# Attention and mixture-of-experts kernel: inputs stored with a column of ones for the second matmul, all turned operands copied by VectorE

## The reference

```python
xh = x.reshape(B, T, H, hd)                          # H = 16 heads, hd = 8
x_centered = xh - jnp.mean(xh, axis=1, keepdims=True)
corr = softmax(einsum('bthd,bThd->bhtT', x_centered, x_centered))
out = einsum('bhtT,bThd->bthd', corr, xh)            # second matmul, uses x uncentred
x = _layernorm(x + out)
...                                                  # routing: 8 of 64 experts per token
x = _layernorm(x + experts(x) + shared_expert(x))
```

## Time and profile before

| | |
|---|---|
| median of 3 runs | 610.99 us |
| the profiled execution's own time | 613.51 us |
| its span, first to last instruction | 611.4 us |
| TensorE matmul busy | 414.1 us (68%), 2948 instructions |
| VectorE busy | 344.1 us (56%), 1127 instructions |
| ScalarE busy | 382.1 us (62%), 515 instructions |
| GpSimd busy | 374.4 us (61%), 401 instructions |

### The profile page before, as it was taken

The page is one execution under the profiler, slowest core; times in us unless marked ns, Lnnn a source line. Parts: engine busy times, 40 slices in busy tenths (PEclk is TensorE's granted clock), DMA queues, the critical chain, the costliest instruction groups (busy, mean ns, idle before and its releaser), DMA issues.

```text
span 611.4 us, 8799 instructions
## 1 busy us (share of the span) xinstructions
PE 414.1 (68%) x2948; PEld 196.6 (32%) x2948; DVE 344.1 (56%) x1127; ACT 382.1 (62%) x515; POOL 374.4 (61%) x401
## 2 busy tenths in 40 slices
PE   4798899899898998998997974255065656632000
PEld 4323233233333333333332312243064545521000
DVE  5422767777687686796783565864034333332075
ACT  2599899998998998998999972013043222210046
POOL 3000003777776776767767777777707888888755
PEclk9699999999999999999999995567568677566555
DMA  3699991101000000000000000000066555333597
GB/s 103 182 242 292 222 234 43 58 23 26 12 12 19 7 21 8 3 21 6 3 20 6 2 20 2 20 1 2 1 191 122 89 88 63 35 34 35 69 303 213
DMA packets 83122, 43.64 MB, mean 71 GB/s; under 512 B 13319, under 2 KB 82707, under 8 KB 83072
## 3 DMA queue, kind: packets, MB, share of 16 engines
q1 hardware_dynamic: 61568, 36.18, 23.3%
q0 software_dynamic: 21504, 6.81, 9.7%
HBM read 21.27 MB, written 44.40 MB: 107 GB/s over the span
## 4 chain that ended last, share of the span: by engine, by line
PE 27%; POOL 25%; ACT 21%; issue 13%; DVE 9%; DMA 4%; SPq 0%; ACTq 0%; DVEq 0%; POOLq 0%
ACT large L898 15%; POOL sums L511 15%; POOL records L493 10%; PE PV L663 8%; PE S L649 6%; PE M L567 3%; ACT OT L883 2%; PE PV L673 2%; PE M L555 2%; PE M L596 1%; DMA sums<-centred,target 1%; ACT LR L876 1%; PE S L567 1%; PE M L590 1%; DVE last_stats L1487 1%
## 5 line engine op out<-in xcount | busy, mean ns | idle before, releaser
L493 POOL DMA_INDIRECT records<-rec,index x256 | 253.3, 990 | 183.1 <-DVE index L1297 106.5
L898 ACT ACTIVATE large<-S,shift_now 128x1024 f32<-128x1024 f32 x256 | 275.0, 1123 | 25.0 <-PE S L649 24.2
L663 PE MATMUL PV<-large,V 128*9 128x512 f32 x1024 | 134.8, 599 | 0.2 <-ACT large L898 0.2
L511 POOL DMA_INDIRECT sums<-centred,target x64 | 99.5, 1554 | 36.4 <-issue 18.9
L649 PE MATMUL S<-LR 64*128 64x512 bf16 x512 | 99.8, 392 | 20.4 <-ACT large L898 17.4
L649 PEld LDWEIGHTS S<-LR 64*128 64x128 bf16 x512 | 24.2, 93 | 158.4 <-ACT large L898 121.5
L1154 DVE COPY LR<-M 128x1024 bf16<-128x1024 bf16 x42 | 28.7, 684 | 23.5 <-PE M L567 23.5
L1454 DVE CAST target<-number 128x4 uint32<-128x4 f32 x16 | 2.7, 171 | 62.9 <-DMA sums<-centred,target 62.0
L795 PE MATMUL PV<-ident,AK 128*128 128x128 f32 x32 | 9.2, 383 | 42.7 <-DVE AK L1429 42.6
L963 ACT COPY AK<-S 128x512 f32<-128x512 f32 x16 | 9.3, 583 | 44.8 <-PE S L777 44.8
L1002 ACT ACTIVATE last_log<-last_moments,eps 128x4 f32<-128x4 f32 x8 | 2.4, 297 | 45.9 <-DVE last_moments L1490 45.9
(11 more groups left out here) (181 smaller groups left out, 703.8 us busy)
## 6 DMA issues: line engine op xcount, KB each, us to landing
records<-blank SPq DMA_DIRECT2D x1, 6176.0 KB, 29.7
X<-records SPq DMA_DIRECT2D x16, 386.0 KB, 3.6
large<-sums SPq DMA_DIRECT2D x24, 256.0 KB, 4.4
sums<-blank SPq DMA_DIRECT2D x2, 2112.0 KB
large<-L_ffn_w_dram SPq DMA_DIRECT2D x2, 2048.0 KB, 18.9
records<-rec,index POOLq DMA_INDIRECT x256, 2.1
X<-L_attn_x_dram SPq DMA_DIRECT2D x8, 256.0 KB, 2.7
sums<-Z SPq DMA_DIRECT2D x8, 256.0 KB
```

The source lines that it names most:

```text
L493: pool.indirect_dma_start(records, bass.IndirectOffsetOnAxis(ap=index[:, i * TOP + k:i * TOP + k + 1], axis=0), rec[:, i, :], None, bounds ...
L511: pool.indirect_dma_start(sums[n % SUMS], bass.IndirectOffsetOnAxis(ap=target[:, u, i:i + 1], axis=0), ye[:, u, i, :], None, bounds_check= ...
L663: mm = pe.matmul(PV[g % 2][32 * i:32 * i + VCOLS, :], V[:, 2 * c + k, QUAD * g + i, :], E[:, u % 2, i, k, :], start=c == 0 and k == 0, sto ...
L898: nc.scalar.activation(E[:, u % 2, 2 * (i // 2):2 * (i // 2) + 2, i % 2, :], S[:, 2 * (n % 2):2 * (n % 2) + 2, :], ACT.Exp, bias=shift_now ...
```

## The change

X gets nine columns per head instead of eight and is laid out as tile, column, head: a head's eight channels are 16 words (64 bytes) apart. The ninth column, of ones, is filled once by GpSimd. The host passes the input with channels ordered by column and head, so the load still moves 512 contiguous bytes per row. V, its two copies per batch and its waits are gone: `weigh` takes its stationary operand from X, nine words 64 bytes apart. VectorE's two instructions that read X, the subtraction of the mean (L1093) and the addition to O (L1157), read it through the view `by_head`, whose neighbouring words are 64 bytes apart. lr3 and lr6 are copied by VectorE.

```diff
-ACT_TAKES = {3: 11, 6: 15}
...
-        X = sb("X", [P, BATCHES * TILES * DIM])
-        V = sb("V", [P, TILES, HEADS, VCOLS])
+        X = sb("X", [P, BATCHES * TILES * VCOLS * HEADS])
...
+        def inputs_of(q):
+
+            return X[:, q * TILES * VCOLS * HEADS:(q + 1) * TILES * VCOLS * HEADS].rearrange(
+                "p (i c h) -> p i c h", i=TILES, c=VCOLS)
+
+        def by_head(q):
+
+            return inputs_of(q)[:, :, 0:HD, :].rearrange("p i c h -> p i h c")
...
-            fill(V[:, :, :, HD:VCOLS], 1.0)
+            fill(X[:, :].rearrange("p (i c h) -> p i c h", c=VCOLS, h=HEADS)[:, :, HD, :], 1.0)
...
-                    mm = pe.matmul(PV[g % 2][32 * i:32 * i + VCOLS, :], V[:, 2 * c + k, QUAD * g + i, :],
+                    mm = pe.matmul(PV[g % 2][32 * i:32 * i + VCOLS, :], inputs_of(b)[:, 2 * c + k, :, QUAD * g + i],
...
-                v.tensor_tensor(xc[:, :].rearrange("p (i d) -> p i d", i=TILES),
-                                tokens_of(X, q).rearrange("p (i d) -> p i d", i=TILES),
-                                M[bank][:, 0:DIM].unsqueeze(1).to_broadcast([P, TILES, DIM]),
-                                ALU.subtract).then_inc(read[bank], 1)
+                v.tensor_tensor(xc[:, :].rearrange("p (i h c) -> p i h c", i=TILES, c=HD), by_head(q),
+                                M[bank][:, 0:DIM].rearrange("p (c h) -> p h c", c=HD).unsqueeze(1)
+                                .to_broadcast([P, TILES, HEADS, HD]), ALU.subtract).then_inc(read[bank], 1)
...
-                                            tokens_of(X, p), ALU.add))
+                                            O[:, :, :].rearrange("p i (h c) -> p i h c", c=HD), by_head(p), ALU.add))
...
                     post_shared_out(phase, b, p)
+                if with_prep:
+                    take_turned(phase, b, 3)
+                if with_post:
                     post_record(p, t)
...
                 if with_prep:
+                    take_turned(phase, b, 6)
                     take_turned(phase, b, 7)
```

More of the change, by code:

```diff
@@ L257, in post_norm_block @@
         pv_read = sem("pv_read")
-        v_built = sem("v_built")
         shift_taken = sem("shift_taken")
@@ L384, in _ @@
                     sp.wait_ge(x_loaded, 16 * q)
-                sp.dma_start(tokens_of(X, q).rearrange("p (i d) -> p i d", i=TILES),
+                sp.dma_start(inputs_of(q)[:, :, 0:HD, :].rearrange("p i c h -> p i (c h)"),
                              x[q].rearrange("(i p) d -> p i d", p=P)).then_inc(x_loaded, 16)
@@ L554, in mean @@
                 for i in range(TILES):
-                    mm = pe.matmul(M[m][:, 0:DIM], mean_w[:, :], tokens_of(X, q, i, 1), start=i == 0, stop=i == TILES - 1)
+                    mm = pe.matmul(M[m][:, 0:DIM], mean_w[:, :],
+                                   inputs_of(q)[:, i, 0:HD, :].rearrange("p c h -> p (c h)"), start=i == 0, stop=i == TILES - 1)
                 mm.then_inc(written[m], 1)
@@ L657, in weigh @@
                 if k == 0:
-                    if u in (0, UNITS - 2):
-                        wait_next(pe, v_built, 2 * b + (1 if u == 0 else 2))
                     if c == 0 and (g >= 2 or not isinstance(b, int) or b > 0):
@@ L865, in exp_logits @@
                                      ).then_inc(read[bank], 1)
[L867 to L876, removed]
             def copy_quad(b, g):
@@ L906, in batch @@
                                 copy_quad(b - 1, QUADS - 1)
[L907 to L918, removed]
                     if phase != "first":
@@ L1156, in post_norm @@
             def post_norm(p, t):
-                t.step("y", v.tensor_tensor(O[:, :, :].rearrange("p i d -> p (i d)"), O[:, :, :].rearrange("p i d -> p (i d)"),
-                                            tokens_of(X, p), ALU.add))
+                t.step("y", v.tensor_tensor(O[:, :, :].rearrange("p i (h c) -> p i h c", c=HD),
+                                            O[:, :, :].rearrange("p i (h c) -> p i h c", c=HD), by_head(p), ALU.add))
                 t.after("y")
@@ L1507 @@
     for name in _INS:
-        a = np.ascontiguousarray(inputs[name])
+        a = inputs[name]
+        if name == "L0_attn_x":
+            a = np.reshape(a, (BATCHES, TOKENS, HEADS, HD)).transpose(0, 1, 3, 2).reshape(BATCHES, TOKENS, DIM)
+        a = np.ascontiguousarray(a)
         arrays[f"{name}_dram"] = a
```

## The result

The changed kernel takes 614.26 us (median of 20 runs, 611.76 to 617.01) beside 611.39 us for the kernel before (20 runs). The ratio is 1.0047 with a 95% interval of 1.0035 to 1.0060: it is slower by 2.9 us, as forecast (+3.6). The profiled execution has a span of 613.9 us (before: 611.4). In the profiles after, exponential n, A and the slots are named as before.

A forecast was written before the change was run, and what follows sets the result against it. ScalarE and TensorE were taken to bound it in turn, then VectorE's own order. 0.15 us without strides plus 3.5 us for strides gave +3.6 on 610.99, 614.6 us; likeliest 613 to 616.5, 8 in 10 within 609 to 617.

The forecast's parts named there:

- Exponential 1 to A: Up to ScalarE's release of VectorE, after which VectorE runs its own order: first V copy's removal saves 0.40 us, second's nothing.
- Strides: VectorE's two readings of X 64 bytes apart: each 0.53 us longer, 0.49 on the path per batch, 3.5 us in all.
- `most` at A+11.51, the scores of exponential 26 at A+12.26: After VectorE's release by ScalarE: `most` starts 0.76 us late behind lr3's copy; exponential 26 begins 0.1 us later.
- A to the next `mean`: From ScalarE's release of VectorE onward: +0.69 us, 0.53 from lr3's place and 0.16 from lr7 behind lr6.
- A middle batch: Whole middle batch of the attention: 0.29 us longer before strides, +0.78 us with them.
- The weight loads: TensorE's loads of nine strided words: taken as 0, staying near 88 ns; high end 0.3 us a batch.
- Batch 0: First attention batch, with no work of a batch before it and VectorE free: -1.18 us.
- The end: GpSimd's scatters of batches 5 to 7: 0.32 us of slack before batch 6's closes; +0.15 us overall without stride costs.
- Free strides: Rival for VectorE's strided readings: no cost, 611.1 us, no measurable change; chance 0.34 with partial stride costs included.
- ScalarE's time reaching the end: Rival at slot 12: lr3's copy precedes `most`, so ScalarE's saving survives, -7 us, 604 us; chance 0.15.
- The strided loads: Rival: TensorE's weight loads pay too, +1.9 us on the forecast, 616.5 us; chance 0.08 shared with the no-lift rival.
- That the change doesn't lift ScalarE at all: Rival: V's 0.40 us per batch is lost too, 617.0 us; chance 0.08 shared with the strided-loads rival.

The follow-up runs named there:

- before_few: Kernel before, with only the first 12 of a batch's 32 scatters issued; batch 43.47 us.
- storage_few: Changed kernel with VectorE's two readings of X contiguous in storage order and only 12 of 32 scatters per batch; batch 43.70 us.
- two_layouts: Kernel before, with the second matmul's weights taken from a second SBUF layout of the input, loaded by DMA, and V gone; 608.68 us, ratio 0.9953.
- y_few: Changed kernel with 12 of 32 scatters per batch and only the addition to O reading X contiguously; batch 43.70 us.
- lr7_first_few: Changed kernel with 12 of 32 scatters per batch and VectorE copying lr7 before lr6; batch 43.91 us.
- lr3_back: Changed kernel with the copy of lr3 back on ScalarE; 611.58 us, ratio 1.0001.
- layout_only: Changed kernel with the copies of lr3 and lr6 back on ScalarE, leaving only X's layout changed against the kernel before; 611.08 us, ratio 0.9998.
- packed_few: Changed kernel with 12 of 32 scatters per batch and nine neighbouring words of X as the second matmul's weights; batch 43.98 us.
- copies_only: Kernel before, with only the copies of lr3 and lr6 moved to VectorE; 614.41 us, ratio 1.0042.
- after_few: Changed kernel with only the first 12 of a batch's 32 scatters issued; batch 44.05 us.

## Why the prediction was right, point by point

- *Exponential 1 to A, -0.40 us.* Right: 20.21 to 19.83 without strides (0.38 us), in before_few against storage_few and again in two_layouts. Both V copies are gone and no more than the first one's 0.40 us came, so the second gave nothing, as forecast.
- *Strides, +0.53 us, 0.49 on the path.* The mechanism is right, the size too large: 0.35 to 0.37 us, and 0.35 on the path, where I had 0.49. The step that was mis-sized is the 2.1 ns taken from L1139 for each place. 512 words at 64 bytes cost 0.37/512 = 0.7 ns more than neighbours, nearer to the 0.5 ns of L1169 that I set aside as too few words. (A piece of L1139 is eight words of bf16, so its 2.1 ns were not the price of the jump alone.) That the subtraction is covered was right (y_few). Its 0.53 us in the prologue can't be read from these traces, since the first copy of the shift starts anywhere from 16.85 to 18.67 us in them.
- *`most` at A+11.51, the scores of exponential 26 at A+12.26.* Measured 184.15-172.58 = 11.57 and 184.84-172.58 = 12.26. The saving of lr3's copy became a wait of 0.76 us there, and exponential 26 began at A+12.69 instead of A+12.50, 0.19 us late where I had 0.1 (0.12 without meetings: 12.63 beside 12.51).
- *A to the next `mean`, +0.69 us.* Measured +0.60 without GpSimd's meetings and +0.56 as run. I split it 0.53 and 0.16. The 0.16 for lr7 behind lr6 is right (lr7_first_few, and lr3_back beside layout_only); lr3's place costs 0.42 to 0.45. Without meetings VectorE reads `most` 0.60 us later, as I had it (from A+12.84 to A+13.44), but lr5 comes only 0.44 us later (from A+16.68 to A+17.12) where I had 0.53. The batch that I had read also held a long `wsum` (0.43 us at 183.05), which I took for VectorE's own work; in the changed kernel it is short in batches 3 to 6, which gives a part of the delay back.
- *A middle batch, +0.78 us with strides.* Measured +0.56 (0.58 without meetings). What I had too much is 0.14 us for the stride and 0.1 us from the last point.
- *The weight loads, 0.* They took 101 ns instead of "near 88", and packed_few prices that at 0.07 us per batch, well below my high end of 0.3.
- *Batch 0, -1.18 us.* From its first copy of the shift to the `mean` of batch 1: 42.53 us after, 43.55 before, -1.02, in one execution each, both with a granted clock of 0.50 from 20 to 30 us.
- *The end.* GpSimd's first scatter of batch 5 comes at 321.42 us, 2.92 later than before. That the 0.32 us of slack ahead of batch 6's closes is seen in copies_only and lr3_back, where its first scatter starts 0.30 us behind the one before it. It closes in the changed kernel too, but there the last scatter of batch 5 had waited 1.21 us for a DMA. The last scatter of all ends at 445.59 us beside 442.27: +3.3, where I had +3.6. What comes behind it is 168.3 us long beside 169.2 before and 167.8 to 169.1 in the other kernels with all scatters, whatever their change.
- *What I did not have* is VectorE and GpSimd meeting: batch 2 of the changed kernel is 0.74 us longer by it, batch 4 of the kernel before 0.26. In this profiled execution it makes up for the strides that I priced too high, so a part of the closeness of +3.6 to +2.9 is luck. How many batches meet in the timed runs the profile of one can't say.
- *The rivals.* Free strides fall by 1056 ns instead of 691. ScalarE's time reaching the end falls at `most`, which waited 0.81 us for VectorE. The strided loads are real but small. That the change doesn't lift ScalarE at all falls by two_layouts, which gained the 0.38 us.

## What to carry to other kernels

When two engines are both nearly full, work taken off the busier one counts only up to the next wait that ends on another engine. Ask what the copy is next in line for: here ScalarE released a PSUM bank at the right moment, and VectorE, less busy on average, let `most` begin 0.8 us late, because the copy came behind 10 us of its own order. And look at the start of each period for a job that stands ahead of what the other engine waits for; moving one such job gave 0.7 us per batch, where removing both V copies gave 0.38. And before two traces are compared, see whether an instruction between the marks is longer in one of them: `wsum` alone had mixed up the prices of lr3 and lr6.

## What the runs showed of the hardware

TensorE's granted clock in batch 0 isn't the same in every execution. From 20 to 30 us it was 0.50 (1.2 GHz) in the profiles before and after and 1.00 (2.4 GHz) in after_few, whose instructions up to there are the changed kernel's. The rows of the changed kernel and then of after_few:

```profile
20.00:25.00 5.00, 3.58 (x14) 2.05 (x14) 1.37 (x2) 1.98 (x2) 0.00 (x0) 0.50 0.60 175
25.00:30.00 5.00, 4.29 (x20) 0.61 (x24) 3.51 (x9) 3.94 (x5) 0.00 (x0) 0.50 1.10 264
```

```profile
20.00:25.00 5.00, 2.86 (x22) 1.58 (x26) 2.79 (x5) 3.71 (x4) 0.00 (x0) 1.00 0.67 206
25.00:30.00 5.00, 4.69 (x40) 1.14 (x38) 3.22 (x8) 5.00 (x6) 0.00 (x0) 1.00 1.10 261
```

In both, TensorE has been idle for 2.6 us before the first scores (at 20.94 and 20.56 us). Batch 0 took 41.57 us at the one level and 38.96 at the other. These 2.6 us are as large as the effect studied here: single profiled spans of these kernels can't be compared, their middle batches can.

The meetings of VectorE and GpSimd were the other thing I had not expected: 0.13 to 0.28 us on each `tensor_scalar` or cast that starts 0.53 to 0.84 us into GpSimd's period of 1.28 us, up to 0.76 us per batch (44.46 beside 43.70) by phase alone.
